# Causal groups: another release for the loads, another order for the row maxima

## The reference, cut to what matters

```python
Q, K, V = (proj(W_q), proj(W_k), proj(W_v))          # 16 heads of 16
scores = jnp.einsum('bhqd,bhkd->bhqk', Q, K) * DK ** (-0.5)
scores = jnp.where(causal, scores, -jnp.inf)
attn = jax.nn.softmax(scores, axis=-1)
out = jnp.einsum('bhqk,bhkd->bhqd', attn, V)
```

## Time and profile before

| | us |
|---|---|
| median of three runs (2084.05 to 2084.23) | 2084.21 |
| profiled execution, whole | 2087.22 |
| its span, first to last instruction | 2085.5 |
| causal stage in it, first maximum to last store | 132.1 to 662 |
| from the copy of one shift to the next, 14 times, in its middle | 31.1 to 31.5 |

### The profile page before, as it was taken

How to read it: one execution, slowest core, us unless ns; L and a number is a source line. 1 busy time by engine, 2 the same in 40 slices (tenths; PEclk the granted TensorE clock), 3 DMA queues, 4 the chain that set the end, 5 groups by cost and what they waited for, 6 DMA issues and landing times. The chain is left out here.

```text
span 2085.5 us, 41715 instructions
## 1 busy us (share of the span) xinstructions
PE 1868.5 (90%) x12960; PEld 1331.2 (64%) x12960; DVE 1525.0 (73%) x4128; ACT 1209.6 (58%) x2501; POOL 956.1 (46%) x797
## 2 busy tenths in 40 slices
PE   5778999999996899999996999689999999699975
PEld 4633333333332688888875888578888887578875
DVE  5667888888881899999985554389999998555424
ACT  3414666666665677777774444267777777444423
POOL 3441222222122577777762333267777776233310
PEclk9868999999998899999998999889999999899988
DMA  5690554554532000000022121300000002212137
GB/s 198 230 190 17 78 73 59 75 73 60 74 47 67 10 29 26 25 25 25 25 66 63 31 60 55 96 14 26 25 25 25 25 25 65 63 31 60 51 124 244
DMA packets 150662, 134.67 MB, mean 65 GB/s; under 512 B 31298, under 2 KB 133118, under 8 KB 150398
## 3 DMA queue, kind: packets, MB, share of 16 engines
q1 hardware_dynamic: 149182, 131.75, 27.0%
q10 hardware_dynamic: 1344, 1.31, 0.3%
HBM read 86.60 MB, written 46.16 MB: 64 GB/s over the span
## 5 line engine op out<-in xcount | busy, mean ns | idle before, releaser
L636 ACT ACTIVATE ca_pr<-ca_pS 128x1024 f32<-128x1024 f32 (+3 forms) x384 | 302.0, 814 | 222.3 <-PE ca_pS L551 178.3
L895 ACT ACTIVATE w_pe<-w_sm,w_nmax 128x256 f32<-128x256 f32 x512 | 253.4, 497 | 140.3 <-DVE w_nmax L1007 140.2
L826 POOL TENSOR_TENSOR w_tsn<-w_qk,w_tab 128x512 f32<-128x512 f32 x124 | 251.9, 2053 | 162.7 <-DVE w_pn L1016 162.7
L470 POOL TENSOR_SCALAR_AFFINE_SELECT ca_pr<-ca_pr 128x256 f32<-128x256 f32 x256 | 104.1, 408 | 402.6 <-ACT ca_pr L636 399.6
L527 PE MATMUL ca_pR<-ca_ks,ca_qs 96*128 96x512 bf16 (+3 forms) x768 | 238.3, 347 | 32.0 <-DVEq L719 13.1
L662 DVE CUSTOM_DVE_ANT_0 ca_masked<-ca_pR,ca_later 128x256 f32<-128x256 f32 (+3 forms) x512 | 237.1, 485 | 35.4 <-PE ca_pR L527 30.7
L527 PEld LDWEIGHTS ca_pR<-ca_ks,ca_qs 96*128 96x128 bf16 x768 | 68.0, 97 | 227.0 <-DVE ca_mx L662 128.6
L1007 DVE CUSTOM_DVE_ANT_0 w_sm<-w_pS,masks 128x256 f32<-128x256 f32 x512 | 185.8, 420 | 20.9 <-PE w_pS L1191 20.9
L666 DVE TENSOR_REDUCE ca_mx<-ca_pR 128x1 f32<-128x512 f32 x256 | 176.0, 688 | 32.6 <-PE ca_pR L527 30.9
L551 PE MATMUL ca_pS<-ca_qs,ca_ks 98*128 98x512 bf16 (+3 forms) x768 | 189.4, 330 | 5.3 <-issue 3.5
L834 POOL TENSOR_TENSOR w_rs<-w_ssc,mhalf 128x16 f32<-128x16 f32 x64 | 187.9, 2935 | 5.4
(11 more groups left out here) (166 smaller groups left out, 4426.6 us busy)
## 6 DMA issues: line engine op xcount, KB each, us to landing
QKP<-p_parts SPq DMA_DIRECT2D x32, 384.0 KB, 2.9
ca_qs<-QKP SPq DMA_DIRECT2D x96, 128.0 KB, 6.5
ca_ks<-QKP SPq DMA_DIRECT2D x96, 128.0 KB, 6.8
w_xt<-X SPq DMA_DIRECT2D x64, 128.0 KB, 2.0
X<-w_x SPq DMA_DIRECT2D x64, 128.0 KB, 1.7
f_hh<-X SPq DMA_DIRECT2D x32, 256.0 KB, 4.9
f_xr<-X SPq DMA_DIRECT2D x16, 512.0 KB, 4.8
X<-f_x SPq DMA_DIRECT2D x16, 512.0 KB, 3.3
```

The costliest lines, as they stand in the source:

```text
L636: act.activation(pr[:, k % 2, pair, :, 0:w], pS[:, pair, :, 0:w], ACT.Exp, scale=CS).then_inc(p_ready, 1)
L826: pool.tensor_tensor(*sines(w, j, z), ALU.mult).then_inc(S["ts_ready"], 1)
L895: ins = act.activation(pe_[:, h], sm[:, n], ACT.Exp, bias=nmax[:, n:n + 1], scale=-1.0, accum_out=sums[:, h:h + 1])
```

## The change

`PER` becomes 6, 3, 6, 3, 6, 4, 5, 3, 3, 0, 0, 0 (39 instead of 41), `EARLY` 9 maxima in steps 9, 10 and 11 (4, 2, 3) instead of 7 in steps 10 and 11 (3, 4), and each step has its own pair of cuts in `PLACES`. SP issues the loads at the head of a group, when the last scores of the group before (which read the buffer last) are done, and no longer behind the store of its output. The number of instructions is the same; lines behind L507 stand one lower in the changed file.

```diff
-    PER = [6, 5, 4, 4, 5, 5, 5, 5, 2, 0, 0, 0]
-    EARLY = {10: (0, 3), 11: (3, 7)}
-    A, B = 2, 3
+    PER = [6, 3, 6, 3, 6, 4, 5, 3, 3, 0, 0, 0]
+    EARLY = {9: (0, 4), 10: (4, 6), 11: (6, 9)}
+    PLACES = [(2, 3), (2, 6), (2, 3), (0, 1), (2, 4), (0, 3), (2, 3), (1, 7), (3, 8), (3, 3), (5, 5), (2, 6)]
...
             def step(n, u, it, started, more):
                 at, _ = plan(started, more)
+                if n and n - 1 + SLOTS < ITERS:
+                    sp.wait_ge(s_ready, ONE + n * 2 * NSTEP)
+                    load(n - 1 + SLOTS, (u - 1) % SLOTS)
                 for job, kind, half in sum(at, []):
                     if kind == "out":
                         store(n - half, half, n * RJ + job + 1)
                     elif kind == "shift":
                         place_shift((u + 1) % SLOTS, n * RJ + job + 1)
-                    if kind == "out" and half == 1 and not (isinstance(n, int) and n - 1 + SLOTS >= ITERS):
-
-                        load(n - 1 + SLOTS, (u - 1) % SLOTS)
...
                 for k in range(NSTEP):
 
+                    first_ones, next_ones = PLACES[k]
                     scores(n, u, k, 0)
-                    do(at[k][:A])
+                    do(at[k][:first_ones])
                     scores(n, u, k, 1)
-                    do(at[k][A:B])
+                    do(at[k][first_ones:next_ones])
                     if k:
                         weighted(n, u, k - 1)
                     elif started:
                         weighted(n - 1, (u - 1) % SLOTS, NSTEP - 1)
-                    do(at[k][B:])
+                    do(at[k][next_ones:])
```

## The result

| | before | after |
|---|---|---|
| median, us | 2084.22 (2084.05 to 2088.26) | 2071.15 (2068.08 to 2072.98) |
| profiled execution / its span | 2087.22 / 2085.5 | 2068.08 / 2066.3 |
| one group's period in the middle | 31.14 | 30.10 |

What follows compares the result with a forecast made beforehand. No engine is full, so job order decides: DVE paces steps 10 to 5, PE steps 6 to 9, with waits in turn. -13.0 - 1.6 + 1.2 = -13.4 us takes the median 2084.21 to 2070.8; range 2064 to 2081.

Steps and rivals of the forecast that it cites:

- 14 x 0.93 = 13.0: From step 8 of group 0 to step 8 of group 14: 14 periods, each 0.93 us shorter, 13.0 us won.
- The two extra maxima: Ahead of the first shift, where only DVE works: two more 512-wide maxima at 0.61 us each, costing 1.2 us.
- the 1.6 allowed: Steps 0 to 7 of group 0: a gain of at most 1.6 us, all of it taken into the forecast.
- Part 1, the order: Maxima moved from steps 1, 6 and 7, four into step 9: busy time unchanged, period 30.20 us, 0.93 less a group.
- The step table: Forecast lengths: steps 9 to 11 6.90 us, step 0 3.09, 1 to 5 13.07, 6 and 7 4.99, 8 2.15.
- the walk: PE's and DVE's queues carried, job by job, through the new order with three banks: 30.20 us a group.
- Part 2, the shift: Shift moved later in step 9: 1.7 us of slack becomes a 0.25 us stall before step 0, landing 2.6 after the copy.
- Part 3, the loads: Loads at the group's head: cost 0, about 6 us to spare; at the old place about 0.6 us late.
- (a): Steps 9 to 5: DVE keeps the pace, hand-over idles go on; some 2083 us, or 2084 by the PSUM rule; chance 0.12.
- (b): Ahead of step 0: PE's wait for the shift costs more than the order wins; 2098 us; chance 0.04.
- (c): Stall before step 0 brings the half clock back in each group: +14 x 1, 2085 us and more; chance 0.03.
- (d): DVE never dry from step 9 to 5, no stall at the shift: some 29.3 us a group, 2059; chance 0.08.

## Why the prediction was right, and where not

**The time.** 2070.8 was forecast, 2071.15 measured, and the sign and the steps hold. That the two agree to 0.4 us is in part luck. The table's medians differ by 13.1 us, but the ratios say 15.4 to 16.9 us, and the stage itself gained 16.0 us in the traces, not 13.4. The first median of before, 2084.22, is at the low end of what that kernel showed later (2086.8 to 2087.8), which hid the difference.

**Which terms were mis-sized.** The first scores of step 9, in group 0 and in group 14, before and then after:

```profile
192.00 0.50 PE L551 MATMUL ca_pS<-ca_qs,ca_ks 98*128 98x384 bf16 x2
...
628.26 0.50 PE L551 MATMUL ca_pS<-ca_qs,ca_ks 98*128 98x384 bf16 x2
...
188.79 0.50 PE L550 MATMUL ca_pS<-ca_qs,ca_ks 98*128 98x384 bf16 x2
...
610.75 0.50 PE L550 MATMUL ca_pS<-ca_qs,ca_ks 98*128 98x384 bf16 x2
```

These are 14 periods, 436.26 us before and 421.96 after: 14.3 won, where 14 x 0.93 = 13.0 was forecast (the usual period gained 1.04, a few gained less). The difference is spread over all the blocks by 0.1 or less. The two extra maxima cost 1.2, as forecast: from the first maximum to the first shift's copy it is 160.45 - 130.40 = 30.05 instead of 160.91 - 132.08 = 28.83. Group 15 gained 0.1.

Group 0 seems to have gained 2.7 from its first scores to those of its step 9 (164.38 to 192.00 before, 163.90 to 188.79 after), 1.1 more than the 1.6 allowed. But the granted clock did not come back at the same place. Here is the window of the earlier trace rows after, and the one behind it before (the clock is the third number from the end):

```profile
170.00:175.00 5.00, 5.00 (x33) 1.49 (x31) 3.33 (x10) 2.23 (x4) 2.10 (x5) 0.84 0.00 0
...
175.00:180.00 5.00, 4.88 (x45) 1.93 (x42) 4.69 (x18) 2.67 (x6) 1.63 (x4) 0.99 0.00 2
```

Before, shows 0.50 up to 175 and the next window 0.99, so the clock rose at about 175.1, 10.7 us behind the first scores; after, a mean of 0.84 puts it at about 171.6, 7.7 us behind them. The same reading of the other traces (the runs with one DMA for the shift and with the shift in other places agree with the changed kernel's rows: 7.9 to 8.7, and 25.0 to 25.4):

| trace | clock back, behind group 0's first scores | from these to step 9's first scores |
|---|---|---|
| before | 10.7 | 27.62 |
| before, loads moved | 10.1 | 27.42 |
| before, shift later | 8.4 | 26.97 |
| changed | 7.7 | 24.89 |
| changed, again | 8.1 | 25.14 |
| changed, loads put back | 9.8 | 25.90 |

With the clock back at about the same place the change is worth 26.97 - 25.14 = 1.8 or 27.42 - 25.90 = 1.5, so the 1.6 was right, and about 1.1 us of the 16.0 come from where the clock rose in these two traces. Why that place moves from run to run stays open.

**Part 1, the order.** The step table is right to 0.1 everywhere, and the reason is the one given. DVE paces the stretch from step 10 to step 5: relieving steps 6 and 7 without using DVE's idle time in step 9 gave nothing (31.19), and with the four early maxima in step 9 and step 1 down to three, under the same old cuts, it gave 0.25 (30.89). The new cuts without the early maxima of step 9 were not run, so how the 1.04 divides between the two is known with the old cuts only. What the prediction did not say is how much hangs on the cuts: it had them in the walk but named only the counts as what moves. The runs show that counts alone bring 0.25, cuts alone lose 1.25, and both together win 1.04.

**Part 2, the shift.** The stall was forecast at 0.25 and is 0.18; lengthening it by 0.6 costs 0.61 and shortening its issue takes 0.20 off. The landing from the copy's end was 2.53 against 2.6 taken. The fixed cost of about 2.0 us that the Trainium skill ("DMA: Bandwidth & Descriptors", Anatomy of one DMA) gives for one transfer is given there for transfers that GpSimd issues, while SP issues the shift, so it was carried over to another path. From the copy's end it would have had the rows land in time. With two transfers issued in series they did not (2.53). With one, PE stood no longer, so that one landed 2.35 us or less behind the copy's end (317.91 - 315.56); this does not contradict the 2.0, and no run here measures it.

**Part 3, the loads.** At the new place they cost nothing, as forecast. The step that failed is the other half, that the old place would have been 0.6 late: it took the old issue time for the new order, without moving the store ahead of it, which is issued some 1.9 us earlier in a group (the first load 6.8 us into step 0 instead of 8.7). Measured, the old place has 1.1 us to spare. The margin at the new place was put at 6 us and is 9.4, too. There the reader was put at 21.2 after step 0's start, while the prediction's own step table gives 3.09 + 13.07 + 4.99 + 2.15 = 23.3, and it is 23.6 (309.51 - 285.88); by the same table the old place would even have come out 1.3 late (24.6 against 23.3), so the 0.6 was not a consistent reading either. Neither entered the sum, but the first made the first half of the change look needed.

**The rivals.** (a) did not happen: DVE still runs dry in steps 1 to 5 of the new order, 0.78 us at the head of step 2 and 0.30 in step 5, but no more often than the walk had (0.4 to 0.7 twice). The Trainium skill ("Perfetto Trace Analysis", Optimization Strategy) says that consistent bubbles can mean too little PSUM. No run here changes the number of banks, so whether more of them would help is not shown; but with the same three banks the order alone took a third off the wait for them, 7.9 to 5.1, so the 2084 that was read out of this rule is refuted. (b), a shift 0.6 us later still, cost what it was priced at, one for one (0.61). (c) did not happen: the granted clock is 1.00 from 195 to 600 us in both traces. (d) did not happen; its second half, no stall at the shift, is worth 0.20.

## What to carry to other kernels

Where two engines hand work over through a small ring, count per stretch what each has to do, and look for the stretch in which the fuller one idles: here moving work there paid, and moving it elsewhere did not. How many jobs stand in a step and where they stand in it are one decision: here cuts made for other counts were worse, by 1.25 us a group, than one and the same cut for every step. When a step of a chain is moved later, ask what its slack was; here an estimated 1.7 us of slack turned into a stall of 0.2, and one DMA instead of two took it away. And before a gain in a stretch with a changing clock is put down to the change, compare where the clock rose in each trace.

## What I had not expected of the hardware

Two DMAs of 8 KB from one queue land 0.6 us apart in what waits for them (three instead of two: 0.61 more; one instead of two: the stall of 0.18 gone), as long as SP's issue of each (1.20 for two). The 13 loads of a group, 1.8 MB, moved under quite different steps changed no step by more than 0.01 us. And over the fourteen traces the granted clock came back between 7.7 and 10.7 us behind group 0's first scores, which alone makes this group up to 1 us shorter or longer.
